# DLRM tower in one core: the low parts of four tables split one piece a step and taken by ScalarE, and another order of the last tiles

## The reference

```
e = jnp.stack([tbl_0[ids[:, 0]], ..., tbl_31[ids[:, 31]]], axis=1)      # [2048, 32, 256]
iu, ju = jnp.triu_indices(32, k=1)
z = jnp.einsum('bnd,bmd->bnm', e, e)[:, iu, ju]                         # 496 dots
h = jnp.concatenate([z, dense_ctx], axis=1)                             # [2048, 512]
h = jnp.maximum(h @ W_top1 + b_top1, 0.0)                               # 512
h = jnp.maximum(h @ W_top2 + b_top2, 0.0)                               # 256
y = h @ W_top3                                                          # 1
```

## Time and profile before

| what | us |
|---|---|
| median of 3 runs (604.75 to 606.4) | 605.2 |
| the profiled execution: its own time | 607.6 |
| its span | 605.8 |
| busy in it: PE / DVE / ACT / GpSimd | 528.5 / 277.2 / 217.3 / 432.1 |

### The profile page before, as it was taken

The page is one execution under the profiler, slowest core; times in us unless marked ns, Lnnn a source line. Parts: engine busy times, 40 slices in busy tenths (PEclk is TensorE's granted clock), DMA queues, the critical chain, the costliest instruction groups (busy, mean ns, idle before and its releaser), DMA issues.

```text
span 605.8 us, 24947 instructions
## 1 busy us (share of the span) xinstructions
PE 528.5 (87%) x11450; PEld 464.4 (77%) x11450; DVE 277.2 (46%) x604; ACT 217.3 (36%) x423; POOL 432.1 (71%) x463
## 2 busy tenths in 40 slices
PE   1458998999989898998899989998988898998997
PEld 0234795998979797887888788887968788796776
DVE  2002753827454555536354554626455461715143
ACT  1223234344333434333333433342343333333442
POOL 6776577777777777777777777777777777777720
PEclk9999999999999999999999999999999999998999
DMA  5588453343434343433434343343434333333310
GB/s 145 190 232 229 122 151 108 110 126 108 124 107 122 111 125 110 124 109 106 124 108 122 111 125 109 109 126 108 122 108 122 110 108 110 110 107 108 106 47 1
DMA packets 26411, 72.10 MB, mean 119 GB/s; under 512 B 8426, under 2 KB 9338, under 8 KB 25680
## 3 DMA queue, kind: packets, MB, share of 16 engines
q0 software_dynamic: 21888, 59.80, 35.1%
q1 hardware_dynamic: 4420, 10.72, 5.7%
HBM read 70.48 MB, written 0.01 MB: 116 GB/s over the span
## 4 chain that ended last, share of the span: by engine, by line
PE 65%; DMA 13%; POOL 12%; issue 7%; ACT 1%; DVE 1%; SPq 0%
PE ps_l L327 18%; PE ps_turn L243 15%; DMA rows<-in_table,index 13%; POOL rows L230 12%; PE ps_gram L294 12%; PE ps_pick L272 6%; PE ps_pick L274 6%; PE ps_l L341 2%; PE ps_l L258 1%; PE ps_l L361 1%; PE ps_pick L258 1%; PE ps_l L349 1%; DVE pairs L604 0%; PE ps_wide L281 0%; PE ps_gram L311 0%
## 5 line engine op out<-in xcount | busy, mean ns | idle before, releaser
L230 POOL DMA_INDIRECT rows<-in_table,index x456 | 431.3, 946 | 147.3 <-issue 116.4
L461 ACT COPY cols<-ps_turn 128x512 f32<-128x512 f32 x221 | 128.3, 589 | 324.1 <-PE ps_turn L243 323.6
L604 DVE COPY pairs<-ps_gram 32x112 f32<-32x112 f32 (+1 forms) x484 | 181.5, 375 | 128.6 <-PE ps_gram L294 122.4
L243 PE MATMUL ps_turn<-identity,rows 128*128 128x128 f32 x912 | 148.0, 291 | 53.1 <-DMA rows<-in_table,index 52.3
L243 PEld LDWEIGHTS ps_turn<-identity,rows 128*128 128x128 f32 x912 | 102.4, 145 | 74.0 <-DMA rows<-in_table,index 51.2
L294 PE MATMUL ps_gram<-cols 128*32 128x32 f32 x7936 | 109.6, 201 | 18.8 <-issue 17.2
L294 PEld LDWEIGHTS ps_gram<-cols 128*32 128x32 f32 x7936 | 90.0, 111 | 44.4 <-issue 39.7
L591 DVE TENSOR_TENSOR one_hot<-ps_wide,row_number 125x2048 fp32r<-125x2048 f32 x28 | 63.9, 2281 | 122.8 <-ACT ps_wide L478 102.5
L272 PE MATMUL ps_pick<-one_hot,table_hi 125*128 125x256 f32 x448 | 114.3, 293 | 0.4 <-ACT stage L482 0.4
L327 PE MATMUL ps_l<-pairs,w_sb 128*128 128x128 f32 x960 | 109.9, 276 | 0.7 <-DVE score L623 0.7
L274 PE MATMUL ps_pick<-one_hot,table_lo 125*128 125x256 f32 x448 | 109.6, 283 | 0.0
(11 more groups left out here) (68 smaller groups left out, 144.4 us busy)
## 6 DMA issues: line engine op xcount, KB each, us to landing
rows<-in_table,index POOLq DMA_INDIRECT x456
pick_id<-in_pick_ids SPq DMA_DIRECT2D x14, 250.0 KB
w_sb<-in_w_t SPq DMA_DIRECT2D x1, 2048.0 KB, 23.5
cols<-in_tbl SPq DMA_DIRECT2D x2, 1000.0 KB
stage<-in_tbl SPq DMA_DIRECT2D x2, 1000.0 KB
w_sb<-in_W_top SPq DMA_DIRECT2D x1, 512.0 KB, 26.7
pairs<-in_dense_t SPq DMA_DIRECT2D x16, 8.0 KB, 2.1
scores<-score SPq DMA_DIRECT2D x16, 0.5 KB
```

Source lines behind the costliest of these rows:

```text
L230: pool.indirect_dma_start(out=rows[x % ROWS][:, k, :], out_offset=None, in_=table, in_offset=bass.IndirectOffsetOnAxis(ap=index[:, t, i:i ...
L243: last = pe.transpose(ps_turn[x % TURNS][:, h, SPG * k:SPG * (k + 1), :], rows[x % ROWS][:, k, h * P:(h + 1) * P], identity[:, :])
L461: act.copy(cols[t % COLS][:, :, :, FPU * u:FPU * (u + 1)], ps_turn[x % TURNS][:, :, :, :]).then_inc(cols_ready, 1)
L604: last = dve.tensor_copy(pairs[n % 2][N_FIELDS * q:N_FIELDS * (q + 1), c0:KC, per * j + s0:per * j + s0 + FQ] .rearrange("p c g -> p g c") ...
```

## The change

Five things, all in the kernel's own order of work:

- The raw tables lie elsewhere: table 0 in `stage` buffer 0, tables 1, 2 and 3 one after the other in `stage` buffer 1. SP issues the weight loads when table 0 has landed, table 2 when 8 pieces are made (tables 0 and 1 split), and table 3 when 12 are.
- `split_table` becomes `split_piece`: a unit has at most one piece. Pieces 0 to 3 stand at (1,4) to (1,7), 4 to 7 at (2,0) to (2,3), 8 to 11 at (3,1) to (3,4), 12 at (3,7), 13 to 15 at (4,0) to (4,2). A piece waits until the one before it has been taken.
- `take_lo` moves from DVE to ACT, behind the evacuation of the piece's unit. `make_hi` stands ahead of the evacuations of (1,3), (1,7), (3,0) and (3,6).
- The first 64 samples of the last tile go through `partial_layer1` too (64 wide, two sums under each other, a second fold matrix `fold2`), in place of the four strips.
- Layer 2 of tile 13 moves from (30,0) to the end of (29,6), and four of five spins go.

```diff
+    def piece(t, u):
+        if t == 1 and u >= 4:
+            return u - 4
+        if t == 2 and u < 4:
+            return PIECES + u
+        if t == 3 and 1 <= u <= 4:
+            return 2 * PIECES + u - 1
+        if t == 3 and u == ALL - 1:
+            return 3 * PIECES
+        if t == BPG and u < 3:
+            return 3 * PIECES + 1 + u
+        return -1
...
+        table_raw = [stage[g][0:VP, :, :, :].rearrange("p h s j -> p (h s j)").rearrange("p (c d) -> p c d", c=VC)
+                     for g in (0, 1, 1, 1)]
...
             sp.wait_ge(table_loaded[0], 16)
-            load_table(2)
-            sp.wait_ge(table_loaded[1], 16)
             sp.dma_start(w1_sb[:, :, :], w1_t).then_inc(w1_loaded, 16)
...
-            sp.wait_ge(low_done, 3 * PIECES)
-            load_table(3)
+            for j in (2, 3):
+                sp.wait_ge(low_done, j * PIECES)
+                load_table(j)
...
+            def split_piece(x):
+                j, i = x // PIECES, x % PIECES
+                if i == 0:
+                    pe.wait_ge(hi_ready, j + 1)
+                if x >= 1:
+                    pe.wait_ge(lo_ready, x)
+                if x == 2 * PIECES:
                     pe.wait_ge(stage_ready, 2)
...
-                        pe.wait_ge(lo_ready, PIECES * (3 if j < 2 else 4))
+                        pe.wait_ge(lo_ready, PIECES * (4 if j >= 2 else j + 1))
...
-            def first_layer1(m0, m1):
...
+            def partial_layer1(i):
+                if i == 0:
+                    pe.wait_ge(pairs_ready, BLOCKS - 1)
+                    pe.wait_ge(late_pairs_ready, 2)
+                    pe.wait_ge(dense_loaded[(TILES - 1) % 2], 16 * TILES // 2)
+                    pe.wait_ge(hidden1_ready, TILES - 1)
+                else:
+                    pe.wait_ge(half_pairs_ready, 2 * i)
+                width = BLOCK if i == 0 else N_FIELDS
+                strips = P // width
                 for c in range(KC):
-                    j = c % QUAD
+                    j = c % strips
...
-                    if t == 1 and u in (4, 5, 6):
-                        split_table(u - 4)
-                    if t == 3 and u == 6:
-                        split_table(3)
+                    if piece(t, u) >= 0:
+                        split_piece(piece(t, u))
...
-                    if t >= 4 and t % 2 == 0 and u == 0:
+                    if 4 <= t < BLOCKS - 2 and t % 2 == 0 and u == 0:
                         layer2((t - 4) // 2)
+                    if t == BLOCKS - 3 and u == 6:
+                        layer2(TILES - 3)
...
+            def take_lo(x):
+                j, i = x // PIECES, x % PIECES
+                act.wait_ge(low_done, x + 1)
+                act.copy(table_lo[:, j, :, :].rearrange("p c d -> p (c d)")[:, 512 * i:512 * (i + 1)],
+                         ps_low[0 if x < 2 * PIECES else 1]).then_inc(lo_ready, 1)
...
-                    if t == 1 and u in (4, 5, 6):
-                        make_hi(u - 4)
-                    if t == 3 and u == 6:
-                        make_hi(3)
+                    if (t, u) in ((1, 3), (1, 7), (3, 0), (3, 6)):
+                        make_hi({(1, 3): 0, (1, 7): 1, (3, 0): 2, (3, 6): 3}[t, u])
                     evacuate(t, u)
+                    if piece(t, u) >= 0:
+                        take_lo(piece(t, u))
```

More of the change, by code:

```diff
@@ L151, in dlrm_tower, with part @@
         stored = [sem(f"stored{p}") for p in range(2)]
-        def first(x):
-            return x[:, 0:BLOCK]
-        def part(x, half):
-            return x[:, BLOCK + N_FIELDS * half:BLOCK + N_FIELDS * (half + 1)]
+        def part(x, i):
+            return x[:, 0:BLOCK] if i == 0 else x[:, BLOCK + N_FIELDS * (i - 1):BLOCK + N_FIELDS * i]
         block = ctx.enter_context(nc.Block())
@@ L562, in _ @@
             regroup_half_upper(1)
[L563 removed]
             act.wait_ge(l2_done, TILES - 1)
[L565 to L578 removed]
+            for i in range(3):
+                act.wait_ge(summed, i + 1)
+                for m in range(M1C if i < 2 else M1C // 2):
+                    rectified = act.activation(part(hidden1[:, m, :], i), ps_sum[i][m], ACT.Relu, bias=b1_sb[:, m:m + 1])
+                rectified.then_inc(last_hidden1_ready, 1)
         @block.vector
@@ L638, in regroup_half, with take_partial @@
                 last.then_inc(half_pairs_ready, 1)
-            def take_partial(half):
-                dve.wait_ge(partial_done, half + 1)
-                dve.tensor_copy(partial[half], ps_partial[half]).then_inc(partial_ready, 1)
+            def take_partial(i):
+                dve.wait_ge(partial_done, i + 1)
+                dve.tensor_copy(partial[i], ps_partial[i]).then_inc(partial_ready, 1)
             for p in range(2):
@@ L683, in _ @@
             regroup_half(0)
+            take_partial(0)
             take_score(TILES - 2)
-            take_partial(0)
+            take_partial(1)
             regroup_half(1)
-            take_partial(1)
-            dve.wait_ge(summed, 2)
-            for m in range(2, M1C):
-                last = dve.tensor_scalar(part(hidden1[:, m, :], 1), ps_sum[1][m], b1_sb[:, m:m + 1],
+            take_partial(2)
+            dve.wait_ge(summed, 3)
+            for m in range(M1C // 2, M1C):
+                last = dve.tensor_scalar(part(hidden1[:, m, :], 2), ps_sum[2][m], b1_sb[:, m:m + 1],
                                          0.0, ALU.add, ALU.max)
```

103 lines of the change are left out of this document (26 added, 77 removed).

## The result

| | before | after |
|---|---|---|
| median us (lowest to highest), 6 runs each | 605.33 (604.26 to 607.43) | 621.69 (620.97 to 623.02) |
| profiled execution, its span | 607.6, 605.8 | 620.97, 619.2 |
| last gather starts | 579.08 | 596.09 |
| last gather to the end of the span | 26.7 | 23.1 |

The ratio is 1.0261, 95% interval [1.0239, 1.0284]: 16.4 us slower by the medians. The direction was forecast; the size (+7.6) was less than half of it, and 621.69 lies just outside the range of 602 to 621.

What follows compares the result with a forecast made beforehand. GpSimd's gathers (2.5 us a unit) set the pace up to the end; the tail is PE's own work. Head +15.4 and tail -7.8 gave +7.6 on a median of 605.2: 612.8 us, range 602 to 621.

Steps and rivals of the forecast that it cites:

- the three waits of before: GpSimd's longer waits for transposes where PE splits tables 0 to 2: 6.6 us in all, forecast to go.
- time lost at unit 26: Block 3, where (3,0) is unit 24: with table 2 issued only at 69.6, transposed at 94.4, due 88.7; 5.7 us lost.
- further loss up to unit 32, half clock: Unit 32 is (4,0): table 3 waits for piece 11, PE idles, its clock falls; loss grows from 5.7 to 14.0 us.
- in blocks 4 and 5 behind it: Pieces 13 to 15, layer 2, pick halves and tile 1's layer 1 before unit 41 raise the loss from 14.0 to 22.
- lost in all in the head: GpSimd's gathers up to the last: 22.0 us lost against 6.6 before, so +15.4 us.
- rival (a): Table loads in the head come faster, landing in 7.4 us: 604.5 us; chance 10%.
- (b): Head: w1 doesn't hold up units 6 to 9, PE is early, piece 11 done before 88: 599.8 us; chance 11%.
- (c): Head: no stall is left at all, which needs a table in under 5 us: 590.8 us; chance 5%.
- first term of the tail: Tail: PE waits for rows again, so (31,6) starts at 582.4 instead of 588.99: -6.6 us.
- its other term: Tail: from (31,6) to the last layer 2 takes 10.4 us where it was 11.6: -1.2 us.
- partial 1.8: Tail, behind (31,6): the first partial on the way to the last layer 2, taken as 1.8 us.
- Rival (d): Tail: with four spins fewer, a gap of 1.9 us at (31,3) may lower PE's clock: 615 to 622 us; chance 14%.

Runs made afterwards that it cites:

- own3: After, but raw table 3 has its own buffer and is issued right behind table 2, not behind piece 11: 606.9 us, ratio 1.002 to before.
- all4: Own3, but all four raw tables are resident and each is issued when the one before has landed, waiting for no piece: 602.45 us, ratio 0.9937 to before.
- w1_last: All4, but the four tables are loaded first and w1 is issued at 46.62 instead of 22.15: 605.12 us, ratio 1.0001 to before.
- order_only: Before, with layer 2 of tile 13 in block 29 and four spins fewer, but the four strips kept: 603.8 us, ratio 0.9974 to before.
- tail_only: Before, with the whole new end of after: 601.98 us, ratio 0.9919 to before.
- head_only: After, with the whole old end of before: 622.44 us, ratio 1.0269 to before.
- spins_back: After, with three of the four removed spins put back, in (30,5), (30,6) and (31,3): 625.06 us, ratio 1.0304 to before.

## Why the prediction was right in direction and wrong in size

Step by step against the trace of after:

| step of the prediction | forecast | trace |
|---|---|---|
| w1 goes out, PE's last wait for rows | 22.9, near 47 | 22.77, 44.01 |
| piece 7 starts | 68.3 | 66.64 |
| the three waits of before | gone | gone |
| table 2 has landed; piece 8 | 82.0; 85.6 | 80.17; 83.65 |
| time lost at unit 26 | 5.7 | 5.4 |
| piece 11 done; table 3 has landed | 100.2; 112.6 | 100.3; 113.23 |
| further loss up to unit 32, half clock | 8.3 | 9.5 |
| in blocks 4 and 5 behind it | 8.0 | 7.4 |
| lost in all in the head | 22.0 | 22.3 |
| last gather | 594.5 | 596.09 |
| last gather to the end | 18.9 | 23.1 |

**The head held.** Every wait is where it was forecast, each by the mechanism named: table 2 behind piece 7, table 3 behind piece 11, conversions ahead of evacuations, half clock after the idle stretch. Own3 shows the mechanism of the largest by taking it away, all4 that of both. Two small errors cancelled: PE was 1.7 us earlier at piece 7, and piece 8 and the layer 1 behind it ran partly at the lower clock (from 83.65 to 85.91 and on to 93.46, 2.26 and 7.55 us, where I took 1.1 and 7.15). The last gather came 1.6 us late, 1.3 of it from 456 gathers of 949 ns instead of 946; that has nothing to do with the change.

**A table takes 12.2 and 12.9 us** here, where I took 12.4; rival (a) with 7.4 is out. The estimate of 9.1 that I had worked out from the Trainium skill's page "DMA: Bandwidth & Descriptors" (Why a DMA increments its semaphore by 16 and not by 1) is too short; the measurement decides.

**Rivals (b) and (c)** needed an early PE or a table in under 5 us. PE was 1.7 us early, not ten. In w1_last the hold-up by w1 moved and didn't go.

**The failed step is the first term of the tail: "PE then waits for rows again instead of running 6.6 us behind them: (31,6) starts at 582.4 instead of 588.99".** That is 3.3 us after the last gather. In after, (31,6) starts 603.72 - 596.09 = 7.6 us after it, where it was 9.9 in before: 2.3 us gained instead of 6.6. The whole tail gained 26.7 - 23.1 = 3.6 us by the prediction's own method, instead of 7.8; its other term held, since from (31,6) to the last layer 2 it is 10.24 us, with 10.4 forecast. In no trace of the eleven kernels with the new order does (31,6) start sooner than 6.4 us behind the last gather (6.69 in order_only and 8.82 in tail_only, both with the old head), so the late head is not the reason.

The step took for granted that PE would be ahead of the rows; I had not added up PE's work in front of (31,6). These are rows of it, in before and in after:

```profile
562.80 3.81 PE L327 MATMUL ps_l<-pairs,w_sb 128*128 128x128 f32 x32 [0.67 <-DVE score L623]
...
570.45 0.60 PE L243 MATMUL ps_turn<-identity,rows 128*128 128x128 f32 x4
...
573.58 1.83 PE L294 MATMUL ps_gram<-cols 128*32 128x32 f32 x128
```

```profile
571.99 1.25 PE L303 MATMUL ps_gram<-cols 128*32 128x32 f32 x85 [1.18 <-issue]
...
574.28 1.12 PE L290 MATMUL ps_wide<-w_sb,identity 128*128 128x512 f32 x2
...
577.31 3.81 PE L337 MATMUL ps_l<-pairs,w_sb 128*128 128x128 f32 x32 [1.46 <-DVE score L616]
...
584.96 1.47 PE L253 MATMUL ps_turn<-identity,rows 128*128 128x128 f32 x12
...
587.25 1.83 PE L303 MATMUL ps_gram<-cols 128*32 128x32 f32 x128 [0.81 <-ACT cols L458]
...
592.09 1.07 PE L303 MATMUL ps_gram<-cols 128*32 128x32 f32 x60 [1.70 <-issue]
...
594.00 2.59 PE L350 MATMUL ps_pick<-hidden,w_sb 128*128 128x128 f32 x16
```

From the transposes of (30,0) to those of (31,6) PE took 588.99 - 550.66 = 38.3 us in before and 603.72 - 567.29 = 36.4 in after. The 1.9 us are made up like this:

1. Layer 2 of tile 13 is gone from there: 3.1 us gained, as forecast.
2. The four spins, 0.86 us each or 3.4 in all, gave back 1.4. They stood for the most part where PE has to wait for another engine in any case. From the spins to the layer 1 of tile 14 it is 562.80 - 559.71 = 3.09 us with two of them, 577.31 - 574.28 = 3.03 with one: the wait for the score grew from 0.67 to 1.46. From the transposes of (30,5) to the next gram part it is 3.13 us with two spins and 2.29 without, since PE now waits 0.81 us for ACT's copy. The fourth gave 0.5. In the traces of all eleven kernels with the new order the wait for the score is 1.4 to 2.0 us.
3. The partial of the first 64 samples gained nothing over the two strips (order_only). The prediction has no duration for it: its "partial 1.8" is that of a quarter behind (31,6), which takes 1.75 us there from start to start. The expectation of order_only takes it for this one by mistake.
4. Lost were 1.2 us in a gram part of block 30 (the gap of 1.18 that ends by "issue") and 1.6 us between 589.60 and 596.43, by a longer gap of this kind (1.70 instead of 1.51) and the lower clock. Such a gap stood in before too (1.51, above), and I had counted PE's work without its gaps.

3.1 + 1.4 - 1.2 - 1.6 is 1.7; the rest is small. The rows of (30,0) also came 0.4 us sooner, counted from the last gather.

**The base itself** was off as well. The 26.7 us come from one execution, 2.3 us above its median, and head_only shows the same old tail in 23.6, with (31,6) 6.8 us behind the last gather instead of 9.9: much of the delay that the change was to take away was that execution's. Against head_only the new tail gains 0.5 us in the traces and 0.75 in the medians, against 4.4 us on the old head. I had moved a median of 605.2 by a difference taken from an execution of 607.6. In the spans the change is 619.2 - 605.8 = 13.4; in the medians it is 16.4, since 607.6 lies 2.3 above the one median and 620.97 lies 0.7 below the other.

Of the miss of 5.8 us in spans, 1.6 are head and 4.2 tail; 3 more in the medians are the base. Whether the new tail really gains less behind a late head, or how much of 4.4 against 0.75 is the scatter of four runs (600.1 to 605.0 in tail_only), isn't settled.

**Rival (d)** (the tail loses its clock, 615 to 622) gave about the right time for a wrong reason: in after the clock cost little (0.69 in one stretch of 5 us, layer 2 in 2.59 instead of 1.95), and putting spins back didn't lower the time. In single executions it cost more (1.6 us in tail_only's trace).

## What to carry to other kernels

A buffer that is used twice ties a load to the work that frees it: count that load's full time from there, and the clock that the waiting TensorE loses on top. Work that only fills a wait gives nothing back when it goes: before counting it as gained, ask what the engine would wait for in its place. A shape that looks like a measured one but uses the array half as densely needs its own duration. And where a gain is a gap in one trace, look whether that execution lies above its median, since the gap may be what put it there.

## What the runs showed of the hardware

- The load of a table of 125 rows (1.02 MB) beside the gathers, from its issue until ScalarE could convert it, took 12.2 and 12.9 us in after, 13.2 and 13.0 in head_only, 13.0 and 13.8 in spins_back (up to 0.9 us apart in the same code), and 13.3 for table 2 in own3, where table 3's load stood right behind it.
- After 1.22 us of idle time before piece 8 the layer 1 behind it took 7.31 us (all4), after 3.46 us 7.71 (after), after 4.53 us 8.52 (own3) and 9.07 (head_only). After 11.34 us the clock was at 0.50 in the whole of 115 to 120, and pieces took 2.07 us instead of 1.02.
- w1's 2 MB land in 22.2 to 23.5 us wherever they are issued (before, after, all4, w1_last), and the waits of 2 us and more for rows on PE end 4 to 22 us behind its issue.
- Runs of gram matmuls on PE show gaps of 0.7 to 2.2 us that end by "issue", 9 to 18 of them between 90 us and the end in each of the thirteen traces, often at the same places of the program. No run tells what they are.
